# Inverse norms of q and k as one power on GpSimd instead of a logarithm and an exponential on ScalarE

## The reference

```
q = q / clip(norm(q over the 64 of a head), 1e-12) * q_scale
k = k / clip(norm(k over the 64 of a head), 1e-12) * k_scale
q, k = rotary_xpos(q, k)
out = softmax(8 * q @ k^T, within windows of 64, each looking one window back) @ v
```

## Time and profile before

| | |
|---|---|
| median of 3 runs | 2486.04 us (2484.22 to 2486.11) |
| the profiled execution's own time | 2478.58 us |
| its span in the profile | 2476.0 us |
| PE busy | 1848.3 us, 75% |
| DVE busy | 1400.1 us, 57% |
| ACT busy | 1345.0 us, 54% |
| POOL busy | 1028.8 us, 42% |
| mean granted TensorE clock | 0.848 of full |

### The profile page before, as it was taken

The page is one execution under the profiler, slowest core; times in us unless marked ns, Lnnn a source line. Parts: engine busy times, 40 slices in busy tenths (PEclk is TensorE's granted clock), DMA queues, the critical chain, the costliest instruction groups (busy, mean ns, idle before and its releaser), DMA issues. The chain is left out here.

```text
span 2476.0 us, 46876 instructions
## 1 busy us (share of the span) xinstructions
PE 1848.3 (75%) x15304; PEld 1147.3 (46%) x15304; DVE 1400.1 (57%) x2403; ACT 1345.0 (54%) x4514; POOL 1028.8 (42%) x947
## 2 busy tenths in 40 slices
PE   4697389997859998874366656647999794899978
PEld 2453266663536666432122222214666552666645
DVE  3343477773467776353244454426877454777735
ACT  2233367775236777431266666625777542777752
POOL 0343277871057786012100000007878402888710
PEclk8798699999969999985555666668999996999999
DMA  1000111001010100102444444101100101100011
GB/s 43 7 1 1 40 27 27 18 19 39 27 28 18 27 23 15 34 1 77 97 46 43 45 42 47 20 28 31 27 23 19 26 18 46 27 23 23 19 35 34
DMA packets 84958, 73.82 MB, mean 30 GB/s; under 512 B 16692, under 2 KB 66952, under 8 KB 84744
## 3 DMA queue, kind: packets, MB, share of 16 engines
q1 hardware_dynamic: 84744, 71.11, 15.3%
HBM read 27.07 MB, written 10.49 MB: 15 GB/s over the span
## 5 line engine op out<-in xcount | busy, mean ns | idle before, releaser
L623 POOL TENSOR_TENSOR rsum<-pa,pb 128x512 f32<-128x512 f32 x256 | 322.2, 1280 | 150.4 <-DVE pa L460 150.4
L553 ACT ACTIVATE ffn_prob<-sc,ffn_nmax 128x128 f32<-128x128 f32 x1024 | 361.1, 387 | 0.0
L614 POOL TENSOR_TENSOR ffn_prob<-ffn_prob,ffn_rden 128x512 f32<-128x512 f32 x256 | 261.2, 1042 | 108.9 <-DVE ffn_rden L493 108.9
L468 DVE TENSOR_TENSOR pb<-proj,ffn_tab 128x512 f32<-128x512 f32 x256 | 175.6, 686 | 198.4 <-ACT rn L544 198.4
L346 PE MATMUL proj<-ffn_wqkv_hi,ffn_hhi 128*128 128x512 f32 x256 | 122.8, 480 | 205.0 <-POOL ffn_hlo L636 200.2
L630 POOL TENSOR_TENSOR rsum<-rsum,ffn_rnt 128x512 f32<-128x512 f32 x256 | 262.1, 1046 | 12.6 <-ACT ffn_rnt L582 12.6
L553 ACT ACTIVATION_READ_ACCUMULATOR ffn_prob<-sc,ffn_nmax 128x1 f32 x1024 | 231.8, 226 | 0.0
L1367 ACT ACTIVATE column_E<-proj,column_nm 128x256 f32<-128x256 f32 x256 | 120.1, 481 | 160.5 <-DVE column_nm L1294 160.5
L483 DVE TENSOR_REDUCE ffn_nmax<-sc 128x4 f32<-128x512 f32 x256 | 164.4, 684 | 51.8 <-PE sc L385 51.8
L544 ACT ACTIVATE rn<-proj 128x512 f32<-128x512 f32 x256 | 140.6, 586 | 96.4 <-PE proj L348 94.3
L1294 DVE TENSOR_REDUCE column_nm<-proj 128x2 f32<-128x512 f32 x128 | 87.8, 686 | 171.3 <-PE sc L1239 170.5
(11 more groups left out here) (197 smaller groups left out, 4520.8 us busy)
## 6 DMA issues: line engine op xcount, KB each, us to landing
ffn_v<-ffn_v SPq DMA_DIRECT2D x128, 128.0 KB, 2.3
column_qs<-qk_parts SPq DMA_DIRECT2D x128, 64.0 KB
column_ks<-qk_parts SPq DMA_DIRECT2D x128, 64.0 KB
rn<-Y SPq DMA_DIRECT2D x32, 128.0 KB, 2.3
qk_parts<-column_hi SPq DMA_DIRECT2D x16, 256.0 KB, 2.1
qk_parts<-column_lo SPq DMA_DIRECT2D x16, 256.0 KB, 2.2
rn<-Y SPq DMA_DIRECT2D x32, 127.5 KB, 2.4
ffn_v<-L_ffn_wqkv SPq DMA_DIRECT2D x4, 768.0 KB
```

The costliest lines, as they stand in the source:

```text
L468: return dve.tensor_tensor(halves(K.m2[:, r, w]), halves(K.proj[w][:])[:, :, ::-1], K.tab[:, t % 2, 2 * w + 1].rearrange("p (a d) -> p a d ...
L553: ins = act.activation(K.prob[:, r, e, k], K.sc[e][:, tokens(k)], ACT.Exp, bias=K.nmax[:, e, k:k + 1], accum_out=K.den[:, r, e, k:k + 1])
L614: pool.tensor_tensor(K.prob[:, r, e], K.prob[:, r, e], K.rden[:, r, e].unsqueeze(2).broadcast_to([P, 4, P]), ALU.mult).then_inc(S.f_pn, 1)
L623: pool.tensor_tensor(K.sm[:, r, w], K.m1[:, r, w], K.m2[:, r, w], ALU.add).then_inc(S.f_sum, 1)
```

## The change

ACT's two instructions per tile go. POOL computes `ssc ** -0.5` in one instruction, for tile `j - 1`, after `normalise` and ahead of `scale`; the exponent is a constant column. `ss16` and `ssc` hold two tiles. DVE's clamp no longer waits for ACT, and its sum of squares waits for the power of two tiles before.

```
@@ DVE: norms(j)
                 dve.wait_ge(S.f_sq, 2 * TILES * n + 2 * j + 2)
-                dve.tensor_reduce(K.ss16[:], K.sq.rearrange(...), AX.X, ALU.add).then_inc(S.f_ss, 1)
+                if j >= 2:
+                    dve.wait_ge(S.f_rn, TILES * n + j - 1)
+                dve.tensor_reduce(K.ss16[:, j % 2], K.sq.rearrange(...), AX.X, ALU.add).then_inc(S.f_ss, 1)
                 dve.wait_ge(S.f_ss, TILES * n + j + 1)
-                if j >= 1:
-                    dve.wait_ge(S.f_ln, TILES * n + j)
-                dve.tensor_scalar(K.ssc[:], K.ss16[:], NORM_MIN, None, ALU.max).then_inc(S.f_cl, 1)
+                dve.tensor_scalar(K.ssc[:, j % 2], K.ss16[:, j % 2], NORM_MIN, None, ALU.max).then_inc(S.f_cl, 1)
@@ ACT: inverse_norms(j) and its call at the end of the step
-                act.wait_ge(S.f_cl, TILES * n + j + 1)
-                act.activation(K.lss[:], K.ssc[:], ACT.Ln, scale=SS_SCALE, bias=K.ssb[:]).then_inc(S.f_ln, 1)
-                act.wait_ge(S.f_ln, TILES * n + j + 1)
-                if j >= 2:
-                    act.wait_ge(S.f_scl, 2 * TILES * n + 2 * (j - 1))
-                act.activation(K.rnt[:, j % 2], K.lss[:], ACT.Exp, scale=-0.5, bias=K.rsb[:]).then_inc(S.f_rn, 1)
@@ POOL: new inverse_norms(j), and its place
+            def inverse_norms(j):
+                r = j % 2
+                pool.wait_ge(S.f_cl, TILES * n + j + 1)
+                pool.tensor_tensor(K.rnt[:, r], K.ssc[:, r], K.mhalf[:].broadcast_to([P, 2 * HEADS]), ALU.pow).then_inc(S.f_rn, 1)
                 if 1 <= i <= TILES:
                     normalise(i - 1)
                 if 0 <= j - 1 < TILES:
+                    inverse_norms(j - 1)
                     scale(j - 1)
                 if 0 <= j < TILES:
                     sums(j)
```

More of the change, by code:

```diff
@@ L34 @@
 MASKED = -1e30
-SS_SCALE = 2.0 ** 40
-SS_BIAS = 2.0 ** -64
 NORM_MIN = 1e-24
@@ L96, in _ @@
             pool.memset(K.eps[:], EPS_LN)
-            pool.memset(K.ssb[:], SS_BIAS)
-            pool.memset(K.rsb[:], float(20.0 * np.log(2.0)))
+            pool.memset(K.mhalf[:], -0.5)
         @block.tensor
@@ L473, in norms @@
                 dve.wait_ge(S.f_sq, 2 * TILES * n + 2 * j + 2)
-                dve.tensor_reduce(K.ss16[:], K.sq.rearrange("p w (h d) -> p (w h) d", d=DH), AX.X, ALU.add).then_inc(S.f_ss, 1)
+                if j >= 2:
+                    dve.wait_ge(S.f_rn, TILES * n + j - 1)
+                dve.tensor_reduce(K.ss16[:, j % 2], K.sq.rearrange("p w (h d) -> p (w h) d", d=DH), AX.X, ALU.add).then_inc(S.f_ss, 1)
                 dve.wait_ge(S.f_ss, TILES * n + j + 1)
-                if j >= 1:
-                    dve.wait_ge(S.f_ln, TILES * n + j)
-                dve.tensor_scalar(K.ssc[:], K.ss16[:], NORM_MIN, None, ALU.max).then_inc(S.f_cl, 1)
+                dve.tensor_scalar(K.ssc[:, j % 2], K.ss16[:, j % 2], NORM_MIN, None, ALU.max).then_inc(S.f_cl, 1)
             def maxima(i):
@@ L574, in keep_values @@
                 act.copy(K.v[:, q % 2, slot(t)], K.ob[:]).then_inc(S.f_ve, 1)
-            def inverse_norms(j):
-                act.wait_ge(S.f_cl, TILES * n + j + 1)
-                act.activation(K.lss[:], K.ssc[:], ACT.Ln, scale=SS_SCALE, bias=K.ssb[:]).then_inc(S.f_ln, 1)
-                act.wait_ge(S.f_ln, TILES * n + j + 1)
-                if j >= 2:
-                    act.wait_ge(S.f_scl, 2 * TILES * n + 2 * (j - 1))
-                act.activation(K.rnt[:, j % 2], K.lss[:], ACT.Exp, scale=-0.5, bias=K.rsb[:]).then_inc(S.f_rn, 1)
             def keep_queries(j):
@@ L604, in _ @@
                     keep_queries(j - 1)
-                if 0 <= j < TILES:
-                    inverse_norms(j)
         @block.gpsimd
@@ L1403, in __init__ @@
         self.f_cl = new("f_cl")
-        self.f_ln = new("f_ln")
         self.f_rn = new("f_rn")
@@ L1517, in ffn @@
         K.v = sb("v", [P, 2, 6, INNER])
-        K.ss16 = sb("ss16", [P, 2 * HEADS])
-        K.ssc = sb("ssc", [P, 2 * HEADS])
-        K.lss = sb("lss", [P, 2 * HEADS])
+        K.ss16 = sb("ss16", [P, 2, 2 * HEADS])
+        K.ssc = sb("ssc", [P, 2, 2 * HEADS])
         K.rnt = sb("rnt", [P, 2, 2 * HEADS])
@@ L1632, in build @@
         K.eps = sb("eps", [P, 1])
-        K.ssb = sb("ssb", [P, 1])
-        K.rsb = sb("rsb", [P, 1])
+        K.mhalf = sb("mhalf", [P, 1])
         K.colp = sb("colp", [P, 3])
```

## The result

The changed kernel took 2684.9 us (2677.87 to 2686.34, 4 runs) against 2486.07 us beside it: a ratio of 1.0795, 95% interval 1.0775 to 1.0815, so 199 us or 8% slower. I had forecast 2484 us and a range up to 2550.

What follows compares the result with a forecast made beforehand. PE was taken to bound plain steps, a chain through low_parts each quartet's start. With a 0.69 us power the ramp gave -1.6 us and quartets 0: 2486.04 - 1.6 = 2484.4, stated as 2484, range 2475 to 2550.

Steps and rivals of the forecast that it cites:

- What bounds the kernel: PE bounds plain steps of 7.66 us; at a quartet's start a chain through low_parts makes PE wait 3.00 us.
- ACT's part: Removing ACT's logarithm and exponential frees 0.63 us of ACT per tile, but gains 0 in a block's later steps.
- The price c: Time of one power on POOL, taken as 0.69 us from ACT's pair; at least 0.12, upper row 3.52.
- The ramp: In 16 ramp steps, norms are on the path: change 16 x (c - 0.79) us, at best -10.7.
- the best end: Cheapest power, c = 0.12: the ramp step gains 0.67 us, -10.7 us over 16 steps, total 2475.
- POOL's knee: POOL bounds quartets from c = 1.61; between 1.07 and 1.61 a backlog costs a microsecond or two per block.
- The size for a dear power: Loss with POOL as bound: c = 2 gives +69 us, 2555; c = 3 gives +213, 2699.
- The recorded line: Time change of ramp plus quartets: 16 x (c - 0.79) + 128 x (c - 1.61) us, the last where positive.
- dear power, slower: Rival: POOL becomes the bound; from c = 1.1 the ramp costs 5 us; chance 0.33, half above c = 2.
- The rule weighed: About 12 cycles per element would make the power's 16 columns 0.16 us over the fixed part, total near 2475.

Runs made afterwards that it cites:

- both moves: Changed kernel with high_parts one step earlier and low_parts in its step but between scale and sums: 2665.94 us, ratio 1.0738.

## Why the prediction was wrong

**What bounds the kernel.** Right. PE in the plain steps, the chain through `low_parts` at the quartet's start, ACT's pair in neither: the multiplication in place of the power left the plain steps at 7.67 us, and taking the chain off PE's path brought 101 us.

**ACT's part at 0 in the later steps.** Right by the same run.

**The price c, the step that failed.** "The row nearest in kind is ACT's pair, ... I take 0.69 us." It measured 2.91. ACT's row says what the function costs on ACT, in two instructions of another kind; it bounds nothing on POOL. The upper row that I used for the range's reasoning, 3.52 us, did contain it and gave +288; but I then cut the range at c = 2 by a chance that rested on no row.

**The ramp.** Wrong in form. Of the 2.7 us per block at the best end 0.6 to 0.9 remained with the multiplication. In its ramps three steps in a row have DVE's clamp at 0.66 to 0.95 us, up to 0.50 before, again ending with one of POOL's instructions; that this takes back the whole rest is likely and was not tested by itself.

**POOL's knee.** "A backlog grows over three plain steps and the quartet's start takes it up again, with a microsecond or two per block lost." At c = 1.02 a block loses 14. POOL's lateness at the quartet's end goes through the clamp into the chain that PE waits for, and the clock falls behind the wait. I had POOL's slack as 0.84 + 0.28 us. Only the 0.84 could be used up: the 0.28 is a wait for the reciprocal behind the clamp, and it moves with the end of `sums`.

**The size for a dear power.** The recorded line with c = 2.91 gives 16 x 2.12 + 128 x 1.30 = +200 us, and +199 was measured. That agreement is luck. The 128 should be 112, and the ramp costs 23 us (4 x 5.8), not 34, which makes 23 + 146 = 169 us. Counted by POOL's work, a quartet needs 27.65 + 4 x (2.91 + 0.14) = 39.85 us instead of 34.09. The measured ones, 20 behind the ramps, are 39.7 to 41.6 us, mean 40.3, and seven times that difference of 6.2 us is 44 of the 46 us that a block lost behind its ramp. So the line left out the 0.14 us behind each power and the half microsecond per quartet over POOL's own work.

The rival "dear power, slower" was thus the right mechanism, with its place (POOL full, PE waiting on `scale`) and nearly its price. What was wrong was its chance, 0.16 above c = 2.

**The rule weighed,** 12 cycles per element in the Trainium skill, GPSIMD Engine Reference, "Elementwise — side-by-side cycle accounting", does not cover a power: 0.157 us per column is an estimated 188 cycles at the page's 1.2 GHz. My sum by that rule was off as well: 0.12 + 0.16 us in the line give 16 x (0.28 - 0.79) = -8 us and 2478, not the best end near 2475.

The lock on the clamp has its rule in the Trainium skill too, and I did not weigh it: SBUF — State Buffer, "SBUF: two separate sides", says of the port pair that DVE and GpSimd share that "whichever ... starts first gets the pair for the whole instruction; the other fully blocks", of DVE's side only for an instruction in a two-port mode or with two inputs in SBUF. The trace agrees where POOL works on 512 columns, by clamps that end 0.03 us behind `sums`, and the kernel without the clamp by its 51 us. It does not agree for the power: in the kernel with two powers 44 clamps ran wholly inside one, in 0.17 to 0.18 us, and the measurement decides.

```profile
445.95 0.18 DVE L475 TENSOR_SCALAR ffn_ssc<-ffn_ss 128x16 f32<-128x16 f32 x1
```
```profile
444.02 2.90 POOL L616 TENSOR_TENSOR ffn_rnt<-ffn_ssc,mhalf 128x16 f32<-128x16 f32 x1
```

## What to carry to other kernels

Before an operation moves to an engine on which no trace shows it, measure that one instruction at two widths; a range from rows of other engines is no price, and a queue with 1.07 us to spare per step cannot take 2.91. An engine's idle time is also smaller than it looks where a second engine's instruction ends with it: look for short instructions whose duration varies and whose ends follow another engine's. And where the profile names a wait that the planned change does not touch, 3.00 us at each of 24 quartet starts here, that wait is the better place to work.

## What the runs showed of the hardware

- A power on POOL costs 0.394 + 0.157 us per column of 128 float32, with the exponent as a broadcast column; a multiplication of 16 columns costs 0.22 us.
- DVE's clamp of 128x16, from SBUF to SBUF, took 0.17 to 1.33 us, and in the kernels before and after every one of 128 ended 0.03 to 0.07 us behind one of POOL's 512-column `tensor_tensor` instructions. Inside a power it took 0.17 to 0.18. DVE's reciprocal of 128x8, SBUF to SBUF too, kept 0.19 to 0.21 us everywhere, also inside `sums`.
- The high-part cast of 128x512 took 0.41 to 0.43 us beside an idle POOL, up to 0.97 with 8 columns of power and up to 1.56 in the changed kernel with both moves. DVE's products that read PSUM, running beside POOL's instructions, stayed at 0.67 to 0.69.
- PE's clock fell to its lower level behind all 20 waits of 3.50 us and the four of 3.6 in the kernel with 4 columns. Behind waits of 3.00 to 3.02 us, in the kernels before, with the multiplication and with 4 columns and no clamp, it fell only at the first starts of a block, never at the last three. But it fell behind 15 of 22 waits of 2.87 us in the kernel with 8 columns, behind 13 of 18 waits of 2.63 in the changed kernel, and there once not behind 3.60. So the length of the wait alone does not decide it; what does is left open.
